# Where the second expert's row is written: by attention, or whole by the first expert pass

## The reference, cut to what matters

```python
h = tok(x, ...)
h = h + attn(_layernorm(h), ...)           # 8 heads of 64, causal within 128 tokens
h = h + ffn(_layernorm(h), ...)
# ffn, for each token
logits = x @ router_w.T + router_b         # 8 experts
topk_val, topk_idx = top_k(logits, 2)
weights = softmax(topk_val)
y_e = (silu(h1_e) * h2_e) @ fc2_w[e].T + fc2_b[e]    # h1_e, h2_e: fc1 of expert e, 2 x 256 wide
out = weights[0] * y_first + weights[1] * y_second
```

## Time and profile before

| | |
|---|---|
| runs, median (lowest to highest) | 1311.32 us (1310.25 to 1314.24) |
| profiled execution, own time | 1309.72 us |
| its span | 1307.9 us |
| PE busy | 1196.9 us (92%) |
| PEld busy | 1027.0 us (79%) |
| DVE busy | 1053.9 us (81%) |
| ACT busy | 955.4 us (73%) |
| POOL busy | 865.8 us (66%) |
| L609, scatters in attention | 256, 1019 ns each on POOL |
| L645, scatters to xs in pass 1 and to out_h in pass 2 | 970 and 964 ns each on POOL |

### The profile page before, as it was taken

One profiled execution on the slowest core, in us unless ns is written; L12 is line 12 of the kernel. 1 busy time (PEld: TensorE's weight loads), 2 busy tenths in 40 slices (PEclk: granted clock), 3 DMA queues, 4 the chain that ended last, 5 costly groups with the idle time before them and its releaser, 6 DMA issues. The chain is left out here.

```text
span 1307.9 us, 47296 instructions
## 1 busy us (share of the span) xinstructions
PE 1196.9 (92%) x13772; PEld 1027.0 (79%) x13773; DVE 1053.9 (81%) x3980; ACT 955.4 (73%) x3352; POOL 865.8 (66%) x1207
## 2 busy tenths in 40 slices
PE   6889899999999999999999999728999997999995
PEld 4577787787877877788788787617999997899995
DVE  6568988888888888888888887747888885888885
ACT  2788899999999899989999998714555553555552
POOL 6335767767767766776776776765677774667775
PEclk8899999999999999999999999959999998999998
DMA  6141111111111111111111111238999997999994
GB/s 186 66 175 47 46 46 38 57 43 39 53 47 39 47 53 39 39 57 41 38 55 43 39 57 44 68 107 275 318 348 349 329 339 230 313 337 345 346 343 164
DMA packets 95043, 184.65 MB, mean 141 GB/s; under 512 B 18236, under 2 KB 42500, under 8 KB 94852
## 3 DMA queue, kind: packets, MB, share of 16 engines
q1 hardware_dynamic: 54404, 63.45, 15.9%
q10 hardware_dynamic: 20736, 75.80, 15.4%
q0 software_dynamic: 19840, 44.62, 9.6%
HBM read 46.45 MB, written 53.18 MB: 76 GB/s over the span
## 5 line engine op out<-in xcount | busy, mean ns | idle before, releaser
L737 ACT ACTIVATE probs<-ps,neg_max 128x128 f32<-128x128 f32 (+1 forms) x1024 | 336.7, 368 | 1.3 <-DVE neg_max L924 1.3
L609 POOL DMA_INDIRECT xs<-normed,row x256 | 260.8, 1019 | 70.5 <-issue 66.7
L737 ACT ACTIVATION_READ_ACCUMULATOR probs<-ps,neg_max 128x1 f32 x1024 | 240.1, 236 | 0.0
L1209 PE MATMUL ps<-xT_hi,w_now 128*128 128x256 f32 x576 | 178.8, 310 | 18.6 <-DVE xT_lo L1094 9.3
L693 ACT ACTIVATE masked<-ps,w_now 128x256 f32<-128x256 f32 x288 | 121.0, 471 | 74.2 <-PE ps L1211 69.2
L557 POOL TENSOR_TENSOR probs<-probs,inv_sums 128x384 f32<-128x384 f32 x120 | 100.1, 834 | 103.9 <-DVE inv_sums L874 103.2
L1211 PE MATMUL ps<-xT_hi,w_now 128*128 128x256 f32 x576 | 163.4, 284 | 0.0
L1210 PE MATMUL ps<-xT_lo,w_now 128*128 128x256 f32 x576 | 163.3, 284 | 0.0
L1123 DVE SCALAR_TENSOR_TENSOR probsT<-ps,w_now,masked 128x256 f32<-128x256 f32 x288 | 126.1, 479 | 43.7 <-PE ps L1211 29.9
L1391 PE MATMUL ps<-w,probsT 128*128 x1152 | 153.4, 276 | 3.0 <-DVE probsT L1123 3.0
L746 ACT ACTIVATE probsT<-ps,rstd_now 128x512 f32<-128x512 f32 x128 | 88.4, 690 | 83.7 <-PE ps L1321 75.0
(11 more groups left out here) (236 smaller groups left out, 3090.0 us busy)
## 6 DMA issues: line engine op xcount, KB each, us to landing
w_now<-w_parts ACTq DMA_DIRECT2D x144, 514.0 KB
v<-xs SPq DMA_DIRECT2D x102, 260.0 KB
kT<-xs SPq DMA_DIRECT2D x34, 260.0 KB
xs<-pad_rows SPq DMA_DIRECT2D x16, 520.0 KB, 3.2
normed<-h SPq DMA_DIRECT2D x32, 256.0 KB, 2.6
xs<-normed,row POOLq DMA_INDIRECT x256, 2.3
w_parts<-in_w SPq DMA_DIRECT2D x1, 2048.0 KB, 9.5
xs<-probs,v POOLq DMA_INDIRECT x108
```

The costliest lines, as they stand in the source:

```text
L609: pool.indirect_dma_start((xs[0], xs_parts)[k], bass.IndirectOffsetOnAxis(ap=row[par][:, k, j:j + 1].bitcast(U32), axis=0), normed2[par][: ...
L737: ins = nc.scalar.activation(probs_p[par][:, half, slots[n]], ps[:, SCORES + half, slots[n]], ACT.Exp, bias=neg_max[par][:, half, n:n + 1] ...
L1209: T.matmul(dst, w_hi_, x_hi_, start=True, stop=False)
```

## The change

Attention writes each token only into list 0. The first pass adds its result in the row buffer itself and scatters the whole row, front half and all, to row TARGET of xs[1]. The second pass then loads whole rows from its first block on, after all scatters of the first pass have landed, and its first transposes stand behind the last block of pass 1 instead of two blocks before its end.

```diff
-        late("scatter", half - 3, 2 * n, 2 * n + 2)
+        late("scatter", half - 3, n, n + 1)
...
-                    for k, j in [divmod(n, GB) for n in range(st[2], st[3])]:
-                        pool.indirect_dma_start((xs[0], xs_parts)[k], bass.IndirectOffsetOnAxis(ap=row[par][:, k, j:j + 1].bitcast(U32), axis=0),
-                                                normed2[par][:, j, 0:(ROW, PART)[k]], None).then_inc(scattered[par][k], 16)
+                    for j in range(st[2], st[3]):
+                        pool.indirect_dma_start(xs[0], bass.IndirectOffsetOnAxis(ap=row[par][:, j:j + 1].bitcast(U32), axis=0),
+                                                normed2[par][:, j], None).then_inc(scattered[par], 16)
...
-                            pool.indirect_dma_start((xs_parts, out)[k],
+                            pool.indirect_dma_start((xs[1], out)[k],
                                                     bass.IndirectOffsetOnAxis(ap=xt[j][:, r, GOES_TO[k]:GOES_TO[k] + 1].bitcast(U32), axis=0),
-                                                    y[j][:, r, 0:(PART, D)[k]], None).then_inc(added[j], 16)
+                                                    xt[j][:, r, (slice(0, ROW), slice(BASE, BASE + D))[k]], None).then_inc(added[j], 16)
...
             for k in range(TOPK):
-                sp.wait_ge(s_trash, 16 * 16)
-                for par in range(2):
-                    sp.wait_ge(scattered[par][k], SW_LEAD + 16 * GB * octets)
                 sp.wait_ge(table_ready, LEAD + k + 1)
-                if k > 0:
-                    for j in range(XBUFS):
-                        load_part(turns, j, 0)
-                    for j in range(XBUFS):
-                        sp.wait_ge(added[j], SW_LEAD + 32 * turns)
-                    for j in range(XBUFS):
-                        load_part(turns, j, 1)
-                with sp.Fori(k * turns + k, (k + 1) * turns) as i:
+                for j in range(XBUFS):
+                    sp.wait_ge(added[j], SW_LEAD + 32 * k * turns)
+                with sp.Fori(k * turns, (k + 1) * turns) as i:
                     for j in range(XBUFS):
                         load_rows(k, i, j)
...
-                    V.tensor_copy(row[par][:, 0], row_f[:, 0])
-                    V.tensor_scalar(row[par][:, 1], row_f[:, 1], 2.0, None, ALU.mult)
-                    V.tensor_scalar(normed2[par][:, :, TARGET:ROW].bitcast(I32), row_f[:, 1].unsqueeze(2), 2.0, 1.0,
-                                    ALU.mult, ALU.add).then_inc(row_ready, 1)
+                    V.tensor_copy(row[par][:], row_f[:, 0])
+                    V.tensor_copy(normed2[par][:, :, TARGET:ROW].bitcast(I32), row_f[:, 1].unsqueeze(2)).then_inc(row_ready, 1)
...
-                    ins = V.scalar_tensor_tensor(y[j][:, r, 0:D], ps[:, YB[j % 2], r * D:(r + 1) * D], xt[j][:, r, WEIGHT[k]:WEIGHT[k] + 1],
+                    ins = V.scalar_tensor_tensor(xt[j][:, r, BASE:BASE + D], ps[:, YB[j % 2], r * D:(r + 1) * D], xt[j][:, r, WEIGHT[k]:WEIGHT[k] + 1],
                                                  xt[j][:, r, BASE:BASE + D], ALU.mult, ALU.add)
...
-            for n in range(2):
-                rows_in(n, 0, n)
             for k in range(TOPK):
                 pe.wait_ge(table_ready, LEAD + k + 1)
+                for n in range(2):
+                    rows_in(k * PH + n, k * turns, n)
```

More of the change, by code:

```diff
@@ L131, in final_steps @@
                                "route_apply", "route_weight", "route_rows")]
-    return steps + [("scatter", 1, 0, 4), ("scatter", 0, 4, 8), ("scatter", 1, 4, 8)]
+    return steps + [("scatter", 1, 0, 4)]
 def first_steps():
@@ L257, in build @@
         rows_f = sb("rows_f", [S, TOPK, GB, EXPERTS]); rows_2 = sb("rows_2", [S, TOPK, GB, EXPERTS]); row_f = sb("row_f", [S, TOPK, GB])
-        row = [sb(f"row{i}", [S, TOPK, GB], I32) for i in range(2)]
+        row = [sb(f"row{i}", [S, GB], I32) for i in range(2)]
         ends = sb("ends", [1, LISTS], I32)
@@ L320, in build @@
         row_ready = led_sem("row_ready"); filled_next = led_sem("filled_next"); token_ready = led_sem("token_ready")
-        scattered = [[sem(f"scattered{par}_{k}") for k in range(TOPK)] for par in range(2)]
+        scattered = [sem(f"scattered{par}") for par in range(2)]
         filled_start = led_sem("filled_start"); ends_ready = led_sem("ends_ready")
@@ L409, in octet @@
                         sp.wait_ge(h2_ready, LEAD + GB * (G + 1))
-                        for k in range(TOPK):
-                            sp.wait_ge(scattered[st[1] % 2][k], SW_LEAD + 16 * GB * (o + (st[1] - st[1] % 2) // 2))
-                            carry_wait(sp)
+                        sp.wait_ge(scattered[st[1] % 2], SW_LEAD + 16 * GB * (o + (st[1] - st[1] % 2) // 2))
+                        carry_wait(sp)
                         sp.dma_start(normed2[st[1] % 2][:, :, BASE:BASE + D], h2[st[1] % 2][:, :, 0:D]).then_inc(h2_stored[st[1] % 2], 16)
@@ L420, in load_rows @@
                 sp.dma_start(xt[j], xs[k][bass.ds(first, BLK)].rearrange("(p r) c -> p r c", r=2)).then_inc(xt_in[j], 16)
[L422 to L430, removed]
             load_codes(0, 0)
@@ L537, in step @@
                     G = 2 * o + i
-                    for k in range(TOPK):
-                        pool.wait_ge(scattered[i % 2][k], SW_LEAD + 16 * GB * (o + (i - i % 2) // 2))
+                    pool.wait_ge(scattered[i % 2], SW_LEAD + 16 * GB * (o + (i - i % 2) // 2))
                     pool.wait_ge(token_ready, LEAD + G)
@@ L801, in _ @@
                 for j in range(XBUFS):
-                    block_of((k + 1) * PH - XBUFS + j, j, experts, last=(k == TOPK - 1 and j >= XBUFS - 2), ahead=(k < TOPK - 1 or j < XBUFS - WBUFS + 1))
+                    block_of((k + 1) * PH - XBUFS + j, j, experts, last=(j >= XBUFS - 2), ahead=(k < TOPK - 1 or j < XBUFS - WBUFS + 1))
         @block.vector
@@ L1035, in apply_norm @@
             def apply_norm(o, i, par):
-                for k in range(TOPK):
-                    dve.wait_ge(scattered[par][k], SW_LEAD + 16 * GB * (o + (i - par) // 2))
+                dve.wait_ge(scattered[par], SW_LEAD + 16 * GB * (o + (i - par) // 2))
                 for j in range(GB):
@@ L1142, in turn @@
             def turn(k, i, before, first=False, last=False):
-                apart = first and k > 0
                 for j in range(XBUFS):
                     n = XBUFS * i + j
-                    if not apart:
-                        base(k, i, j)
+                    base(k, i, j)
                     block_of(n, j)
-                    if apart and j > 0:
-                        base(k, i, j - 1, apart)
                     if j > 0:
@@ L1159, in turn @@
                         make_table(1)
-                if apart:
-                    base(k, i, XBUFS - 1, apart)
-            for n in range(2):
-                rest(n, n)
             for k in range(TOPK):
+                for n in range(2):
+                    rest(k * PH + n, n)
                 turn(k, k * turns, None, first=True)
@@ L1168, in _ @@
                     turn(k, i, i - 1)
-                turn(k, (k + 1) * turns - 1, (k + 1) * turns - 2, last=(k == TOPK - 1))
+                turn(k, (k + 1) * turns - 1, (k + 1) * turns - 2, last=True)
                 give(k, (k + 1) * turns - 1, XBUFS - 1)
@@ L1436, in _ @@
                 for j in range(XBUFS):
-                    block_of((k + 1) * turns - 1, j, last=(k == TOPK - 1 and j >= XBUFS - 2))
+                    block_of((k + 1) * turns - 1, j, last=(j >= XBUFS - 2))
                 n = (k + 1) * PH - 1
```

29 lines of the change are left out of this document (12 added, 17 removed).

## The result

| | median of the runs | range | profiled execution | its span |
|---|---|---|---|---|
| before | 1310.78 us (4 runs) | 1307.89 to 1314.24 | 1309.72 us | 1307.9 us |
| after | 1324.72 us (4 runs) | 1322.67 to 1327.85 | 1326.04 us | 1324.2 us |

The ratio is 1.0112, interval 1.0087 to 1.0137: the change costs 13.9 us where 24.5 were forecast. The profiled executions differ by 16.3 us.

A forecast was written before the change was run, and what follows sets the result against it. Attention was taken as bound by TensorE, both passes by DMA with TensorE close behind. Terms -1 + 19 + 0 + 6.5 + 0 = +24.5 us on 1309.72 us gave 1334.2, as a median 1336 us, range 1318 to 1350.

The forecast's parts named there:

- term 1: Attention: 128 scatters fewer, which TensorE hardly waits for; -1 us, bounds 0 and -18.6.
- term 2: Pass 1: whole-row scatters add DMA time; +17 us over 57 blocks and +2 over 14, together +19 us.
- term 4: Boundary of the passes: pass 2's loads wait for pass 1's last scatter; +6.5 us, from 1.6 to 10.
- term 5: Pass 2: it moves the same bytes as before; 0 us.
- ring rival: Pass 1: DMA has room, eight row buffers set the period; 0.04 us a block, 1320 us in all, chance 0.16.
- bytes rival: Pass 1: the period grows with bytes to 3.08 us, +27, boundary +10; 1348 us in all, chance 0.15.
- the 4 us which the prediction named as a sign against itself: Attention: its end moving more than 4 us earlier would show the prediction wrong; under 2 us was expected.
- the only GpSimd wait that it shows is the 2.3 us: Attention: TensorE's waits name GpSimd's probs scaling for 2.3 us only, so TensorE does not wait for the scatters.
- rival "not slower": Attention: 128 scatters fewer relieve GpSimd's and VectorE's chain, up to -18.6 us; 1297 us in all, chance 0.08.
- Term 3: Pass 1: writing the sum into the row buffer instead of a second buffer costs nothing; 0 us.
- the template: Boundary: priced from the start of pass 1, the same sequence from an empty pipe; eleventh fc2 of pass 2 at 1138.6 us.

The follow-up runs named there:

- late_whole: The changed kernel with attention's 128 scatters put back; 1496.13 us, ratio 1.0030 to the kernel before on the same chip.
- changed_again: The changed kernel itself, unaltered, timed again beside the kernel before on one chip; 1453.19 us, ratio 0.9744.
- whole_2: The changed kernel with attention's 128 scatters put back, timed in a second set of runs; 1489.49 us, ratio 1.0023 to the kernel before.
- changed_3: The changed kernel itself, unaltered, timed once more in the second set of runs; 1444.95 us, ratio 0.9741 to the kernel before.
- late_loads: The kernel before with only the changed kernel's boundary: no pass 2 load, transpose or split ahead of pass 1's last scatter; 1495.02 us, ratio 1.0031.

## Why the prediction was right in its sign and too high by 11 us

The case at 1311 us is meant here; the last column of the account above has the terms. The sum came nearer than its parts: term 1 was off by -3.5 us, term 2 by -2.4, term 4 by -7.0 and term 5 by +4.7. That the last one stands against the others is luck.

*The bound of the passes, and term 2.* This carried the result, and it held: DMA share 0.98, period 2.964 us (2.95 to 3.01 forecast), 0.35 us of all engines a scatter (0.34), q0's part 23.4% (22%). TensorE's share was 0.90, not 0.86; it lay above 2.54 divided by the period before as well (0.96 against 0.94). This rests on two traces and not on an experiment: the kernels meant to prove it ran where stalls hid the bytes. The ring rival as priced (0.04 us a block) is out, since the period rose by 0.27; the bytes rival (3.08 us) too. But the ring's picture is in the trace: blocks go at 2.54 us, with one long gap every seven or eight blocks (4.65 us between blocks 36 and 37, 4.88 between 43 and 44, 4.95 between 51 and 52). So the loss comes once a turn of the eight buffers, as the rival had it; its price is what failed. The Trainium skill, "DMA: Bandwidth & Descriptors", "Where 436 GB/s comes from", has 435 GB/s as the ceiling between buffers on the chip. The pass, a mix of such transfers (the weights) and of rows to and from main memory, ran at 352 GB/s and a share of 0.98, so no such room was there.

*Term 1, -1 us, was mis-sized: -4.45 at the first fc2.* That is past the 4 us which the prediction named as a sign against itself. The step that failed: "the only GpSimd wait that it shows is the 2.3 us". TensorE's waits name the last releaser, and what a scatter delays can reach TensorE through another engine. Right behind the loop of attention the trace shows how. VectorE may write normed2 again only when the scatters that read it have landed. Before, the last of these started at 802.06 us, as the second of a pair:

```profile
804.44 1.12 DVE L1040 TENSOR_SCALAR normed<-h,moments,rstd 128x128 f32<-128x128 f32 x4 [2.70 <-DMA xs<-normed,row]
806.86 0.74 PE L1321 MATMUL ps<-ident,probs 128*128 128x128 f32 x4 [2.43 <-DVE probs L939]
```

and after, where one scatter (798.11 us) stands in place of the pair:

```profile
800.78 1.11 DVE L1014 TENSOR_SCALAR normed<-h,moments,rstd 128x128 f32<-128x128 f32 x4 [1.64 <-DMA xs<-normed,row]
803.23 0.66 PE L1286 MATMUL ps<-ident,probs 128*128 128x128 f32 x4 [1.40 <-DVE probs L918]
```

VectorE waited 1.06 us less for the landing, and TensorE 1.03 us less for VectorE; GpSimd is named in neither. By TensorE's w_o products (L1351, now L1316) the changed kernel was ahead by 1.0 us at 98 us (97.88, now 96.86), 2.0 at 195, 2.6 at the end of the loop (799.79, now 797.18), 4.2 one product later (808.92, now 804.68) and 4.5 at 840. The path of the 1.0 us ahead of 98 us and of the 1.0 us between 98 and 195 stays open, as do 0.6 of the 1.6 us behind the loop. Behind 840 us it gained 1.1 us more, so attention's last such product was 5.6 us earlier (859.04, now 853.47; under 2 us were forecast), but 1.1 us were gone again at the first fc2. At 1486 us the same 128 scatters were worth 36 us (936.84 to 900.80, first fc2 of late_whole and changed_again) and 43 us (whole_2, changed_3), and the kernel became faster by leaving them out. The rival "not slower" had this place, GpSimd relieved of 128 scatters; at 1311 us its price is 4.45 and not 18.6 us, and 3.5 of it lie in the 100 to 840 us from which the 18.6 were read.

*Term 3, in place, 0.* late_whole against late_loads has it together with whole rows: 1 us at 1486, where stalls can hide it. At 1311 it wasn't tried apart.

*Term 4, +6.5 us, was mis-sized: -0.5 at block 82.* At block 74 the boundary had cost 4.0 us (1106.64 before, 1122.79 after, less the 12.11 by which block 71 was late). Then before lost 3.5 and 0.9 us at blocks 80 and 81: 2.56 us in the wait for v<-xs above, and the rest while TensorE, after this pause, ran in part at the lower of its two clock levels (1.2 GHz, matmuls 0.21 us apart in place of 0.12), with 0.62 granted in the mean:

```profile
1123.70:1128.00 4.30, 4.21 (x23) 4.19 (x24) 1.82 (x5) 1.51 (x4) 1.37 (x2) 0.62 0.69 187
```

After lost only 0.7 us there, at block 81. The step that failed is the template, the start of pass 1, taken for a boundary that runs faster. From the end of the last scatter (1105.17) SyncE went on after 1.9 us, where 3.3 + 1.3 = 4.6 were forecast; the first fc2 came 10.7 us after that (12.25); and the next ten blocks took 26.1 us (29.0). In all 38.6 us were measured where 45.8 were forecast, so TensorE stood idle 10.4 us ahead of its first transposes, not 15. Of the first difference 1.3 us are a misreading: the last needed scatter is not the one at 873.26 but the next, at 874.98, so SyncE went on 2.0 us after it, not 3.3. At 1486 us, late_loads puts the whole boundary at 4 to 5 us, with an interval of 1.5 to 7.9.

*Term 5, 0, was +4.7 us.* The step that failed is "moves the same bytes as before, 0". Pass 2 went from 2.654 to 2.731 us a block with the same bytes, DMA at 0.97 in both (1160 to 1290 us: 340 GB/s before, 336 after). Why is open.

*What no step had: the level of 1486 us.* The forecast's chance of 0.92 for slower held where it was measured and fails on the chips at 1486 us. The rows gave no hint: they show no stall of several engines behind GpSimd's scatters.

## What to carry to other kernels

Do not count a GpSimd scatter by its 1 us on GpSimd or its bytes alone: compare the same waits with and without it, and on more than one chip, before a change that trades scatters for bytes is called good or bad. A wait table names the last releaser; an engine that it leaves out can still cost, through the buffer that its transfer holds. An unchanged busy time doesn't say that a stage is unchanged: compare the starts of the same instruction, or count the instructions in the same window. Where a boundary is priced by a template, check each of the template's waits at the place it is meant for, and compare over a stretch long enough that both sides have paid for their reloads.

## What was not expected of the hardware

- The same kernel took 1311 us in one set of runs and 1484 to 1491 us in six others, each on a chip of its own. Single instructions agree (VectorE's sum 344 and 346 ns, the attention scatter 1064 and 1065, here in the changed kernel at 1311 us and in changed_3), and the mean granted clock in attention was 1.00 in both:

```profile
L588 POOL DMA_INDIRECT xs<-normed,row x128 | 136.2, 1064 | 29.5 <-issue 25.1 <-DVE normed L1003 1.7 <-POOL normed L521 1.6
```

```profile
L588 POOL DMA_INDIRECT xs<-normed,row x128 | 136.4, 1065 | 29.0 <-issue 25.6 <-DVE normed L1003 1.7 <-POOL normed L521 1.6
```

  What differs is what happens to the other engines beside rows of scatters: up to 2.9 us of stall for VectorE behind four, and on SyncE, beside twelve, a row of steps of 0.70 us where most take 0.05. Why it is so in six places and was not in the first stays open; no run tells it apart.
- On the chips at 1486 us four scatters to a group of the attention leave it at 25.2 to 25.3 us (24.9 at 1311), eight make it 26.4 to 26.6 (24.9 at 1311).
- Plain stores of whole rows, two a block, ran at 325 GB/s and a share of 0.96, the same bytes as scatters at 352 GB/s and 0.98 in the changed kernel at 1311 us. These are two chips, so the two figures don't compare the two kinds of transfer.
